# A frequency branch in parity halves, with its energy on GpSimd and its join on TensorE

## What is computed

```python
xz = einsum('bld,ed->bel', hidden, in_proj_w)
out   = _mamba_branch(xz, ...)                    # scan forward: 256 channels x 16 states
out_b = _mamba_branch(xz[:, :, ::-1], ...)        # scan backward
x, z = split(xz, 2, axis=1)
xf = fft.fftn(x, axes=(-2, -1))                   # over channels and tokens
xc = concatenate([xf.real, xf.imag], axis=1)      # 512 channels
xc = silu(conv1d(xc, fft_conv_w, 5 taps) + fft_conv_b)
re, im = split(xc, 2, axis=1)
x_out = fft.ifftn(lax.complex(re, im), axes=(-2, -1))
z_out = max(silu(z), axis=-1, keepdims=True)
v = abs(x_out * z_out)
out_f = (v - mean(v)) / sqrt(var(v) + 1e-05)
y = out + out_b[:, :, ::-1] + out_f
return einsum('bdl,od->blo', y, out_proj_w)
```

## Time and profile before

| what | value |
|---|---|
| median of 3 runs (lowest, highest) | 2168.23 us (2166.3, 2169.26) |
| profiled execution: time, span | 2169.9 us, 2168.1 us |
| mean granted TensorE clock | 0.964 of full |
| busy over the whole span: PE, DVE, ACT, POOL | 93%, 78%, 63%, 51% |
| one step of the state-space phase | 84.8 us |

### The profile page before, as it was taken

One profiled execution on the slowest core, in us unless ns is written; L12 is line 12 of the kernel. 1 busy time (PEld: TensorE's weight loads), 2 busy tenths in 40 slices (PEclk: granted clock), 3 DMA queues, 4 the chain that ended last, 5 costly groups with the idle time before them and its releaser, 6 DMA issues. The chain is left out here.

```text
span 2168.1 us, 40611 instructions
## 1 busy us (share of the span) xinstructions
PE 2026.5 (93%) x14620; PEld 1511.3 (70%) x14620; DVE 1685.3 (78%) x2918; ACT 1376.2 (63%) x2687; POOL 1111.9 (51%) x1509
## 2 busy tenths in 40 slices
PE   6999999986999996999999978799999999999879
PEld 5677777754888773777777745577877877877746
DVE  5777777766888875777777766489999999999984
ACT  1677777763777773677777653467586685685633
POOL 3655555613776764555555502345736647556423
PEclk8999999997999996999999998899999999999989
DMA  4656556630000003555565515000000000000000
GB/s 133 150 149 146 147 146 150 151 99 1 2 2 2 2 2 87 148 145 149 145 150 150 144 30 200 0 1 1 1 1 1 1 1 0 1 0 1 1 15 20
DMA packets 147750, 144.94 MB, mean 67 GB/s; under 512 B 14048, under 2 KB 106976, under 8 KB 146912
## 3 DMA queue, kind: packets, MB, share of 16 engines
q1 hardware_dynamic: 127968, 132.91, 22.6%
q10 hardware_dynamic: 19584, 9.44, 2.3%
HBM read 94.07 MB, written 38.80 MB: 61 GB/s over the span
## 5 line engine op out<-in xcount | busy, mean ns | idle before, releaser
L606 DVE TENSOR_REDUCE sb_f_mx<-ps_f_s 128x2 f32<-128x512 f32 x768 | 506.3, 686 | 215.7 <-PE ps_f_s L354 214.6
L530 ACT ACTIVATE sb_f_pt<-ps_f_t 128x1024 f32<-128x1024 f32 x384 | 382.0, 1023 | 113.6 <-issue 56.2
L1942 POOL TENSOR_TENSOR sb_mb_h<-sb_mb_h 128x512 f32<-128x512 f32 x128 | 164.6, 1307 | 305.9 <-DVE sb_mb_h L1827 304.8
L1822 DVE TENSOR_TENSOR_SCAN sb_mb_h<-sb_mb_da,sb_mb_h 128x1024 f32<-128x1024 f32 x128 | 304.4, 2417 | 5.4 <-ACT sb_mb_da L1689 5.4
L354 PE MATMUL ps_f_s<-sb_f_stack 96*128 96x256 bf16 x1536 | 287.7, 280 | 20.2 <-DMA sb_f_stack<-f_scr 12.6
L1503 PE MATMUL ps_mb_f<-sb_mb_fc,sb_mb_cw 128*128 128x256 f32 x1280 | 285.1, 379 | 4.3 <-ACT sb_mb_fc L1702 4.3
L1503 PEld LDWEIGHTS ps_mb_f<-sb_mb_fc,sb_mb_cw 128*128 128x128 f32 x1280 | 238.9, 190 | 38.0 <-ACT sb_mb_fc L1702 6.3
L371 PE MATMUL ps_f_t<-sb_f_stack 128*128 128x256 bf16 x1536 | 233.2, 274 | 4.5 <-ACT sb_f_pt L530 3.3
L1689 ACT ACTIVATE sb_mb_da<-sb_mb_dl,sb_mb_an 128x255 f32<-128x255 f32 x512 | 210.8, 495 | 31.2 <-DVE sb_mb_h L1822 30.7
L354 PEld LDWEIGHTS ps_f_s<-sb_f_stack 96*128 96x128 bf16 x1536 | 140.9, 99 | 108.3 <-issue 43.0
L427 PE MATMUL ps_f_a<-sb_f_pt,sb_f_v 128*32 128x256 f32 x3072 | 187.7, 385 | 1.6 <-ACT sb_f_v L579 1.6
(11 more groups left out here) (250 smaller groups left out, 4145.0 us busy)
## 6 DMA issues: line engine op xcount, KB each, us to landing
f_scr<-sb_f_parts SPq DMA_DIRECT2D x96, 384.0 KB, 2.7
sb_f_stack<-f_scr SPq DMA_DIRECT2D x192, 192.0 KB, 3.1
sb_f_stack<-f_scr SPq DMA_DIRECT2D x192, 128.0 KB, 3.1
sb_f_stack<-f_scr SPq DMA_DIRECT2D x192, 64.0 KB, 3.3
sb_f_stack<-sb_f_mrow ACTq DMA_DIRECT2D x96, 96.0 KB
sb_mb_cw<-in_cw SPq DMA_DIRECT2D x1, 5120.0 KB, 20.0
...
```

Source lines behind the costliest of these rows:

```text
L530: nc.scalar.activation(pt[:, e.two, g, half, :, :], t_bank[i % 2][:, :, :], ACT.Exp).then_inc(s["pt_sb"], 1)
L606: nc.vector.tensor_reduce(mx[:, a.two, half, head:head + 2], s_bank[j % 2][:, :, :], AX.X, ALU.max)\
L1822: nc.vector.tensor_tensor_scan(flat, da[:, un % 2, c, :, :].rearrange("p i n -> p (i n)"), flat, 0.0, ALU.mult, ALU.add).then_inc(s["scan_ ...
L1942: nc.gpsimd.tensor_tensor(hb[:, c, 0:2, :], hb[:, c, 0:2, :], hb[:, c, 2:4, :], ALU.add).then_inc(s["half_sb"], 1)
```

## The change

The first inverse transform is split by the parity of the frequency index. The rows of the convolution's weights, its bias and the transform's matrix are permuted beforehand (`parity`), so that a chunk of 128 rows holds only even or only odd frequencies. The sum over the even ones repeats with half the period, the one over the odd ones repeats with the sign turned; so only half of the output columns are multiplied out, and the two halves of the result are the sum and the difference of the even and the odd part. TensorE makes those parts (the channels picked at every second place, `kc::2`), ScalarE evicts them into `fc`, and GpSimd's new `meet` adds and subtracts them into `uk`. The energy moves from VectorE to GpSimd, `zo` becomes an absolute value on ScalarE, `direct` for the backward direction moves from slot 7 to slot 6, and `join` is dropped: `project_out` multiplies `ys` and `vv` by the same weights into one PSUM sum.

```diff
-                elif slot == 6:
-                    kc = half
-                    if kc == 0:
-                        pe.wait_ge(s["f_sb"], seen + 4)
-                    for c in range(XC_CH):
-                        last = nc.tensor.matmul(f_bank[(1 + kc) % 2][:, :], fs[:, c, kc * P:(kc + 1) * P], gi[:, c, :],
-                                                start=c == 0, stop=c == XC_CH - 1)
-                    if kc == 1:
-                        last.then_inc(s["f_ps"], 1)
+                elif slot == 6 and half == 0:
+                    pe.wait_ge(s["f_sb"], seen + 4)
+                    for kc in range(2):
+                        for odd in range(2):
+                            for ri in range(2):
+                                c = 2 * ri + odd
+                                last = nc.tensor.matmul(f_bank[kc][:, odd * N:(odd + 1) * N], fs[:, c, kc::2],
+                                                        gi[:, c, :].rearrange("p (t a n) -> p t a n", t=2, a=2)[:, :, 0, :],
+                                                        start=ri == 0, stop=ri == 1)
+                    last.then_inc(s["f_ps"], 1)
                 elif slot == 7 and half == 1:
-                    pe.wait_ge(s["f_sb"], seen + 5)
+                    pe.wait_ge(s["uk_sb"], m.b + 1)
...
             def project_out(o, f, m):
-                pe.wait_ge(s["yt_sb"], o.b + 1)
+                pe.wait_ge(s["ym_sb"], o.b + 1)
+                pe.wait_ge(s["vn_sb"], o.b + 1)
...
-                    for c in range(DC):
-                        last = nc.tensor.matmul(w_bank[:, 0, half * P:(half + 1) * P], ys[:, o.parity, c, half * P:(half + 1) * P],
-                                                wop[:, c, :], start=c == 0, stop=c == DC - 1)
+                    for n, t in enumerate((ys[:, o.parity, :, :], vv)):
+                        for c in range(DC):
+                            last = nc.tensor.matmul(w_bank[:, 0, half * P:(half + 1) * P], t[:, c, half * P:(half + 1) * P],
+                                                    wop[:, c, :], start=n + c == 0, stop=n + c == DC)
...
                         direct(m, 0)
+                        direct(m, 1)
...
-                    if m and slot == 7:
-                        direct(m, 1)
...
                     for kc in range(2):
-                        last = nc.scalar.activation(uk[:, kc, :], f_bank[(1 + kc) % 2][:, :], ACT.Copy)
+                        last = nc.scalar.activation(fc[:, 2 * kc:2 * kc + 2, PAD:PAD + N],
+                                                    f_bank[kc][:, :].rearrange("p (c n) -> p c n", c=2), ACT.Copy)
...
                     if o and slot == 0:
+                        act.wait_ge(s["zmax"], o.b + 1)
+                        nc.scalar.activation(zo[:, :], zm[:, :], ACT.Abs).then_inc(s["zo_sb"], 1)
...
-            def energy(o):
-
-                dve.wait_ge(s["f_sb"], FREQ * (o.b + 1))
-                nc.vector.scalar_tensor_tensor(vv[:, :, :], sq[:, :, 0:N], 1.0, sq[:, :, N:2 * N], ALU.mult, ALU.add).then_inc(s["sq2_sb"], 1)
...
-                nc.vector.scalar_tensor_tensor(zo[:, :], zm[:, :], -1.0, zm[:, :], ALU.mult, ALU.max).then_inc(s["zo_sb"], 1)
...
-            def join(o):
...
-                nc.vector.scalar_tensor_tensor(yf[:, :, :], yf[:, :, :], 1.0, vv[:, :, :], ALU.mult, ALU.add)\
-                    .then_inc(s["yt_sb"], 1)
...
+            def meet(m):
+
+                pool.wait_ge(s["f_sb"], m.b * FREQ + 5)
+                v = uk[:, :, :].rearrange("p k (t a n) -> p k t a n", t=2, a=2)
+                eo = fc[:, :, PAD:PAD + N].rearrange("p (k e) (t n) -> p k e t n", k=2, t=2)
+                nc.gpsimd.tensor_tensor(v[:, :, :, 0, :], eo[:, :, 0, :, :], eo[:, :, 1, :, :], ALU.add)
+                nc.gpsimd.tensor_tensor(v[:, :, :, 1, :], eo[:, :, 0, :, :], eo[:, :, 1, :, :], ALU.subtract).then_inc(s["uk_sb"], 1)
+
+            def energy(o):
+
+                pool.wait_ge(s["f_sb"], FREQ * (o.b + 1))
+                since(pool, "o_ps", o.b)
+                nc.gpsimd.tensor_tensor(vv[:, :, :], sq[:, :, 0:N], sq[:, :, N:2 * N], ALU.add).then_inc(s["sq2_sb"], 1)
...
             def step(f, m, o):
+                if o:
+                    energy(o)
                 for un in range(UNITS):
+                    if m and un == UNITS - 2:
+                        meet(m)
```

More of the change, by code:

```diff
@@ L1409, in mamba_phase @@
                  "b_ps", "c_ps", "da_sb", "dbu_sb", "scan_sb", "hc_sb", "half_sb", "hs_sb", "y_ps", "ym_sb", "dd_sb", "dd_ps",
-                 "f_ps", "f_sb", "sq2_sb", "v_sb", "vz_sb", "st_sb", "mv_sb", "sd_sb", "rs_sb", "nm_sb", "vn_sb", "yt_sb", "o_ps", "x_sb"]
+                 "f_ps", "f_sb", "uk_sb", "sq2_sb", "v_sb", "vz_sb", "st_sb", "mv_sb", "sd_sb", "rs_sb", "nm_sb", "vn_sb", "o_ps", "x_sb"]
         s = {n: k.sem(f"mb_{n}", ctx) for n in names}
@@ L1655, in front @@
                     act.wait_ge(s["z_ps"], f.b + 1)
-                    since(act, "yt_sb", f.b - 1)
+                    since(act, "ym_sb", f.b - 1)
+                    since(act, "zmax", f.b - 1)
                     nc.scalar.activation(sz[:, f.parity, :, :], w_bank[:, :, :], ACT.Silu).then_inc(s["sz_sb"], 1)
@@ L1699, in frequency @@
                 elif slot == 1:
+                    since(act, "uk_sb", m.b)
                     for part in range(2):
@@ L1827, in scan @@
                     nc.vector.tensor_tensor(hb[:, c, :, :], hb[:, c, :, :], c_bank[:, :, :], ALU.mult).then_inc(s["hc_sb"], 1)
-            def energy(o):
-                dve.wait_ge(s["f_sb"], FREQ * (o.b + 1))
-                nc.vector.scalar_tensor_tensor(vv[:, :, :], sq[:, :, 0:N], 1.0, sq[:, :, N:2 * N], ALU.mult, ALU.add).then_inc(s["sq2_sb"], 1)
             def strengths(o):
                 n = o.b + 1
+                since(dve, "zo_sb", n - 1)
                 nc.vector.tensor_reduce(zm[:, :], sz[:, o.parity, :, :], AX.X, ALU.max).then_inc(s["zmax"], 1)
-                dve.wait_ge(s["zmax"], n)
-                since(dve, "vz_sb", n - 1)
-                nc.vector.scalar_tensor_tensor(zo[:, :], zm[:, :], -1.0, zm[:, :], ALU.mult, ALU.max).then_inc(s["zo_sb"], 1)
             def spreads(o):
@@ L1873, in combine @@
                 nc.vector.scalar_tensor_tensor(nm[:, :], mv[:, :, 0], -1.0, rs[:, :], ALU.mult, ALU.mult).then_inc(s["nm_sb"], 1)
-            def join(o):
-                n = o.b + 1
-                yf = ys[:, o.parity, :, :]
-                dve.wait_ge(s["vn_sb"], n)
-                dve.wait_ge(s["ym_sb"], n)
-                nc.vector.scalar_tensor_tensor(yf[:, :, :], yf[:, :, :], 1.0, vv[:, :, :], ALU.mult, ALU.add)\
-                    .then_inc(s["yt_sb"], 1)
             def add_output(o):
@@ L1899, in step @@
             def step(f, m, o):
-                if o:
-                    energy(o)
                 for slot in range(UNITS):
@@ L1913, in step @@
                             combine(o)
-                        elif slot == 3:
-                            join(o)
                         elif slot == OUT_SLOT:
@@ L2024, in layout @@
     sin2 = np.sin(2 * np.pi * (np.outer(np.arange(N), np.arange(N)) % N) / N)
+    parity = np.concatenate([np.arange(r * 2 * P + a, (r + 1) * 2 * P, 2) for r in range(2) for a in range(2)])
     rows = lambda m: m.reshape(-1, P, m.shape[1]).transpose(1, 0, 2)
@@ L2071, in layout @@
         "gm": rows(np.concatenate([cos2, -sin2, sin2], 1)).reshape(P, DC, 3, CH_I).astype(f),
-        "gi": rows(inverse).astype(f),
-        "cw": m["fft_conv_w"].transpose(1, 2, 0).reshape(XC_CH, P, FREQ_TAPS, 2 * CH_I).transpose(1, 0, 2, 3),
-        "cb": a["L1_attn_fft_conv_b"].reshape(XC_CH, P).T,
+        "gi": rows(inverse[parity]).astype(f),
+        "cw": m["fft_conv_w"][parity].transpose(1, 2, 0).reshape(XC_CH, P, FREQ_TAPS, 2 * CH_I).transpose(1, 0, 2, 3),
+        "cb": a["L1_attn_fft_conv_b"][parity].reshape(XC_CH, P).T,
         "gate_w": a["L1_ffn_gate_w"],
```

## The result

| what | value |
|---|---|
| changed kernel, median of 4 runs (lowest, highest) | 2196.09 us (2194.59, 2197.9) |
| kernel before, median of 4 runs | 2167.68 us |
| ratio, 95% interval | 1.0127 (1.0114 to 1.0139) |
| profiled execution: time, span | 2196.6 us, 2194.6 us |

The change makes the kernel 28 us slower; the forecast was 2200 us, in a range from 2164 to 2218.

The account below looks back on a forecast made before the run. The prediction took TensorE up to L1522, then ScalarE's queue, as the bound. Six boundaries at 4.9 us (29.5), about +1 for the last and +2 for the tail gave +32.5 on 2168.1: 2200 us, range 2164 to 2218.

Parts of the forecast that it names:

- The bound: Each step is set by TensorE up to L1522, then by ScalarE's queue, with `energy` and the square root in it.
- ScalarE's stretch from the eviction to L1503: At each boundary, ScalarE's work from L1698 to L1503 was to keep its 9.52 us, only starting later.
- GpSimd's queue: At a boundary, `meet` delays `parts`, both halvings and `energy`, which ends at 1762.5 on the earlier trace's clock.
- one GpSimd instruction is held per VectorE instruction with two SBUF inputs: Blocking pattern read from the earlier trace, used to time GpSimd's instructions at the boundary; made `energy` late.
- the boundary: Where one sequence passes into the next: the eviction L1698 starts 4.75 us later, and nothing gives the delay back.
- 0.2 for the clock: TensorE's new waits at each boundary may lower its clock: between 0 and 1.7 us, taken as 0.2.
- 6 x 4.9 = 29.5: The cost in us of the six boundaries laid out alike, the one into the last sequence counted apart.
- the cover: At a boundary, TensorE's second wait covers work slowed after the first; after the second, 0.7 us of cover remains.
- The last boundary and the tail: About +1 us into the last sequence; +2 in the tail from late `energy`, no join and a doubled projection.
- Strided weights: TensorE's weights read at every second element: between nothing and 2.6 us a step, taken as nothing.
- The relief rival: Milder blocking lets `energy` end before 1757.7; 2.3 us gained at each of seven boundaries, 2154 us; chance 0.14.
- The rival of the wait for `meet` itself: TensorE's second inverse waits for `meet`, 0.05 us from doing so; little cost, part of the forecast, no chance of its own.

Follow-up runs that it names:

- e_energy_dve: The changed kernel with only the energy put back on VectorE: 2188.41 us, ratio 1.0087 to the kernel before.
- e_energy_early: The changed kernel with `energy` ahead of `halve(7)` on GpSimd, `meet` still ahead of `parts`: 2182.4 us, ratio 1.0065 to the kernel before.
- e_early_join: The changed kernel with `parts` ahead of `meet`, `energy` ahead of `halve(7)` and the join back on VectorE: 2162.77 us, ratio 0.9974 to the kernel before.

## Why the prediction was right, and where its sizes were off

**The bound was read rightly.** That ScalarE's stretch from the eviction to L1503 follows unchanged: 9.39 us (1773.64 to 1783.03), against 9.52 in the earlier trace rows.

**GpSimd's queue, step by step.** On the clock of the earlier trace rows, 11.09 us taken off: `meet` starts at 1738.5 (laid out 1738.65), `parts` ends at 1747.05 (1747.4), `halve(6)` at 1752.95 (1753.5), `halve(7)` at 1760.8 (1761.2), `energy` at 1762.0 (1762.5), the eviction starts at 1762.55 (1763.1). The rule "one GpSimd instruction is held per VectorE instruction with two SBUF inputs" carried through thirteen GpSimd instructions, six of them held, with an error of half a microsecond. Its slip is in the first: the queue was 0.15 us earlier than laid out, the first cast was issued just before the scan and went through, and the cast and the add behind it were held instead. The number of those held is the same, and so is the sum but for what each had left. The Trainium skill, SBUF — State Buffer, "Who interferes with whom", says that the two exclude each other and the later one blocks fully; the rows agree, 2.27 and 2.53 us beside the scans against 0.39 and 0.66 in the open, the spread of the earlier trace rows again.

**The term that was mis-sized is the boundary.** It was taken at +4.75 us and 0.2 for the clock; it is +4.06 (forecast "6 x 4.9 = 29.5", which is 29.7 by its own 4.95; 24.8 measured). Of the 0.88 us between 4.95 and 4.07, 0.55 is the queue above, 0.13 the stretch to L1503, and 0.2 the clock, which cost nothing here. It did fall: 0.65 and 0.50 from 1764 to 1768. But the wait in front of L1492 was shorter for it (1.31 us, not 3), and ScalarE's time did not move. Where that cover is missing, in e_energy_dve and e_energy_early, the eviction waits 1.8 to 3.4 us for the slowed L1483 at nearly every boundary. The forecast had named both, the cover and a price up to 1.7.

**The last boundary and the tail** were put at +1 and +2. Together they came to +1.95, near the +3, but by terms that cancel, so this agreement is partly luck. The last start of L1701 came 4.05 us later still, as at every other boundary. L1503 then follows 7.2 us behind it instead of 9.5 (in the kernel before, ScalarE waits 2.41 us there for VectorE's `zo`), and up to the first inverse another 1.3 us come back. From the start of the first inverse to that of the second it takes 8.0 us instead of 10.4: the halved transform pays in the tail too, which the forecast left out. From there to the last output addition it takes 23.2 us instead of 19.4, where the forecast had 2 us for all of it; the doubled projection did cost 1.7 of that, as laid out.

**The sum:** 28.9 us at seven boundaries less 2.1 is 26.7 on the phase (706.9 less 680.2), against 32.5 forecast and 26.5 in the span.

**The edits priced at nothing.** Strided weights: 196 ns, nothing on the path. `meet` reading in runs of 128: 1.28 us for each add, as priced from L1942. The relief rival needed `energy` before 1757.7; it fell with GpSimd's 21 us for 11. The rival of the wait for `meet` itself appeared only in e_early_join, at 0.6 us.

**What I had not asked** is which part of the blocking could be avoided. The prediction charged it as a price of the sum on GpSimd; the experiments show that it is one of the order. With `parts` in the time in which GpSimd otherwise waits 8 us, and `energy` ahead of the last halving, the same operations on the same engines make the kernel 0.3% faster, not 1.3% slower.
